# Two buffers each for q and for its pairs, swapped by batch with the scaled nodes and with the raw and turned tiles

## The chip, the cores and the metric

One core of one Trainium2 chip runs the whole program. The metric is the device time of one execution in microseconds. Three executions of the kernel before took 14094.63, 14094.72 and 14200.6 us; their median is 14094.72 us.

## The reference, cut to what matters

```python
# x: (8, 2048, 128), adj: (8, 2048, 2048), all float32
def gnn(x, adj, W, b):                       # layers 0, 2 and 3, up to details of the degree
    d = degree(adj) ** -0.5
    return (d[:, :, None] * adj * d[:, None, :]) @ x @ W + b

def attention(x, adj, WQ, WK, p):            # layer 1
    q, k = x @ WQ, x @ WK
    h = relu(q[:, None, :, :] + k[:, :, None, :])
    score = einsum('bijd,d->bij', h, p)      # 8 x 2048 x 2048 scores, 128 features each
    return softmax(score + where(adj > 0, 0, -1e22)) @ x

x = layernorm(x + layer(x))                  # four times: layer 0, 1, 2, 3
```

The cost is in `h`: for each of the 8 x 2048 x 2048 pairs of nodes, 128 features are added, clipped at zero and summed with the weights p.

## The kernel before, in words

**Layout of the attention.** q of a batch lies in SBUF with the features on the 128 partitions and the 2048 nodes in the row. A "row" of work is one instruction over 128x2048: for one node i, max(q, -k_i) or relu(q + k_i). One block is 128 nodes i (t = 0 to 15 within a batch), cut into 32 groups g of four rows (u = 0 to 3). A place is one group of one block, so a batch has 512 places.

**Two kinds of row.** In 20 of the 32 groups (kind D), VectorE (DVE) takes the max from `q_pair`, in which each 32-bit word holds q as a high and a low float16. In the other 12 (kind A: g = 2, 5, 7, 10, 13, 15, 18, 21, 23, 26, 29, 31), ScalarE (ACT) takes the relu from `q_f32`. Both write to a ring of two groups in `big`. TensorE (PE) multiplies each finished group with a window of weights into the four PSUM banks of `score` (`score_rows`): 32 matmuls of float16 for a D group, 16 of float32 for an A group. DVE and ACT can be at most two groups of their kind ahead of PE. One row of the block, group 1 with u = 3 (`POOL_ROW`), is computed by GpSimd (POOL) in place of DVE, wherever `has_pool_row` says so.

**The end of a block.** After group 31, DVE adds the mask to the four banks and takes the maximum of each (`masked_scores`, L968 and L972). It frees the banks for group 0 of the next block. `masked_at` says where in the next block this stands in DVE's order. ACT takes the exponentials at place 5 (L760); their transposes and the product with x follow at later places.

**Side work.** Into the same order of places the kernel puts, for other batches: the transposition of adj (`raw` is loaded by half rows, PE turns it, ACT copies it to `turned`, SyncE stores it; 32 units, 7 half units each block, from t = 0 on), two sums per half row on ACT (`sum_unit`), the three layers with products of `gs` (the scaled nodes) and pieces of the turned adj (`layer2` from block 2, `layer3` from 6, `layer0` from 10), and q, k and their pairs for the next batch at the end of `layer0` (blocks 11 to 15; stored to DRAM).

**Batches.** A round c runs the attention of batch c + 1, layers 2 and 3 of batch c, and layer 0 and the transposition of batch c + 2. `OPENING` (-2) and `CLOSING` (8 - 1) have side work only, `FIRST` is -1. There are eight rounds with attention, hence seven changes of batch. There `load_q` loads `q_f32` and `q_pair` (1 MB each). All transfers of the program are issued in order by SyncE (SP), which waits on semaphores before each.

**What the change touches.** `load_q` (L530), its call at the end of the round, `load_raw` (L396), `masked_at` and `has_pool_row` with `pool_rows`, `scale_nodes` (L870), and every use of `q_f32`, `q_pair`, `gs`, `raw` and `turned` (those become functions of the round). The functions:

Of the kernel before, what the change touches and what calls it, by code (L numbers as in the profile page):

```python
# [24 lines left out]
def halves(words):  # L25

    return words[:, :].bitcast(F16).rearrange("p (n e) -> p n e", e=2)
# [3 lines left out]
def build(nc, x, adj, w0, b0, wq, wk, p, w2, b2, w3, b3, out):  # L31
# [50 lines left out]
    with ExitStack() as ctx:  # L82
# [8 lines left out]
        q_f32 = sb("q_f32", [P, N])  # L91
        q_pair = sb("q_pair", [P, N])
# [9 lines left out]
        x1_turned, q_new = raw[:, 0:BANK], raw[:, BANK:2 * BANK]  # L102
        k_new = x1_turned
        stage = turned[:].rearrange("p m n -> p (m n)")
        high, pair_new = stage[:, 0:BANK], stage[:, BANK:2 * BANK]
# [6 lines left out]
        w_raw, squares = gs[:, 0, :], gs[:, 2:4, :]  # L112
# [122 lines left out]
        def masked_at(t):  # L235
            return (0, 0) if t == 0 else (1, 1)
# [134 lines left out]
        def _(sp):  # L371
# [23 lines left out]
            def load_raw(c, u):  # L395
                b = c + 2  # L396
                if u == 0:
                    sp.wait_ge(q_stored, qk_step(c + 1, STEPS) * 16)
                    sp.wait_ge(k_stored, qk_step(c + 1, STEPS) * 16)
                    sp.wait_ge(pair_stored, split_of(c + 1, STEPS, 0) * 16)  # L400
                else:
# [3 lines left out]
                sp.dma_start(raw[:], half_rows(b, u)).then_inc(raw_loaded, 16)  # L405
# [52 lines left out]
            def store_qk(c, place):  # L458
                b = c + 2
                for s in qk_at(c, place, "q_store"):  # L460
                    sp.wait_ge(turn_free[1], turn_use(c, ("q", s)) + 1 + AHEAD)
                    sp.dma_start(q_kept[b, :, s * BANK:(s + 1) * BANK], q_new).then_inc(q_stored, 16)
                for s in qk_at(c, place, "k_store"):
                    sp.wait_ge(turn_free[1], turn_use(c, ("k", s)) + 1 + AHEAD)
                    sp.dma_start(k_blocks[:, bass.ds(b * T + s * PER, PER), :],
                                 k_new.rearrange("p (t n) -> p t n", n=P)).then_inc(k_stored, 16)
                for i, what in enumerate(("q_pair_store", "k_pair_store")):
                    for s in qk_at(c, place, what):
                        sp.wait_ge(low_written, split_of(b, s, i) + 1)
                        sp.wait_ge(high_written, split_of(b, s, i) + 1)  # L470
                        if i == 0:
                            dst, src = q_pair_kept[b, :, s * BANK:(s + 1) * BANK], pair_new
                        else:
                            dst = k_pair_blocks[:, bass.ds(b * T + s * PER, PER), :]
                            src = pair_new.rearrange("p (t n) -> p t n", n=P)
                        sp.dma_start(dst, src).then_inc(pair_stored, 16)

            def side(c, place):
                for u in units_where(c, lambda u: evict_place(2 * u + 1) + 1 == place):
                    sp.wait_ge(turn_free[1], turn_use(c, ("unit", u, 1)) + 1 + AHEAD)  # L480
                    store_turned(c + 2, u, turned[:]).then_inc(turned_stored, 16)
# [60 lines left out]
            def attention(c):  # L542
# [15 lines left out]
                if not one_of(c, LAST):  # L558
                    load_q(c + 1)
# [673 lines left out]
```

## Time and profile before

| what | us |
|---|---|
| median of three executions | 14094.72 |
| the profiled execution | 14105.47 |
| its span, first to last instruction | 14103.7 |
| DVE busy | 13362.3 (95%) |
| ACT busy | 13096.3 (93%) |
| PE busy | 13010.3 (92%) |
| POOL busy | 902.7 (6%) |

Three engines are busy for over 90% of the span, so none of them can be read alone: what bounds a stretch has to be found by the stretch. A profile line gives the busy time of a group of instructions and the idle time of its engine before them, with what ended that idle time. A timeline row gives start, length, engine, line and the number of equal instructions merged; the number in square brackets is the idle time before it.

### The profile page before, as it was taken

How to read it: one execution, taken by the hardware profiler on the slowest of the kernel's cores; microseconds unless marked ns; L12 is line 12 of the kernel's file. 1: busy time of each engine (PE TensorE's matmuls, PEld its weight loads, DVE VectorE, ACT ScalarE, POOL GpSimd, SP SyncE). 2: the span in 40 equal slices, each digit the busy share in tenths (PEclk: the TensorE clock that was granted, in tenths of full speed). 3: DMA queues.
4: the chain of work that ended last, by engine and by line, in shares of the span. 5: the costliest groups of instructions: out<-in, count | busy, mean ns of one | idle time of the engine just before them, and what ended most of it. 6: DMA issues, size and time to landing. Idle time of an engine off the chain costs nothing.

```text
span 14103.7 us, 317692 instructions
## 1 busy us (share of the span) xinstructions
PE 13010.3 (92%) x143877; PEld 5491.8 (39%) x143877; DVE 13362.3 (95%) x14048; ACT 13096.3 (93%) x8612; POOL 902.7 (6%) x615
## 2 busy tenths in 40 slices
PE   6889989999899998999989999899989999899988
PEld 3333334443344433443334443344433444333333
DVE  6999999999999999999999999999999999999995
ACT  5999999999999999999999999999999999999994
POOL 0000000000000000001000000000000010000000
PEclk8999999999999999999999999999999999999999
DMA  5111112221122112221122211222112221011103
GB/s 186 45 51 47 49 53 85 86 62 51 55 86 88 61 41 64 88 86 58 40 71 85 86 57 39 73 82 85 60 36 75 89 79 57 30 49 51 43 12 109
DMA packets 714329, 935.45 MB, mean 66 GB/s; under 512 B 61712, under 2 KB 455952, under 8 KB 693520
## 3 DMA queue, kind: packets, MB, share of 16 engines
q1 hardware_dynamic: 712976, 915.13, 20.8%
q8 instruction: 1128, 18.48, 0.5%
q14 instruction: 225, 1.84, 0.0%
HBM read 722.01 MB, written 184.55 MB: 64 GB/s over the span
## 4 chain that ended last, share of the span: by engine, by line
DVE 45%; PE 38%; ACT 13%; issue 2%; DMA 1%; SPq 0%; POOL 0%; DVEq 0%; POOLq 0%; ACTq 0%
DVE big L1019 40%; PE score L1165 28%; ACT big L783 11%; PE acc L1086 5%; PE acc L1145 2%; PE turn L1063 2%; DVE att L968 2%; DVE gx L898 1%; DMA piece<-adj_turned 1%; ACT y_turned L706 0%; ACT turned L696 0%; DMA big<-in_adj_dram 0%; DVE stats L904 0%; PE acc L1092 0%; PE turn L1116 0%
## 5 line engine op out<-in xcount | busy, mean ns | idle before, releaser
L1019 DVE TENSOR_SCALAR big<-q_pair,k_pair_cols 128x2048 f32<-128x2048 f32 x10120 | 12213.0, 1279 | 407.3 <-PE score L1165 391.3
L783 ACT ACTIVATE big<-q_f,k_cols 128x2048 f32<-128x2048 f32 x6144 | 11790.3, 1998 | 297.7 <-PE score L1165 253.1
L1165 PE MATMUL score<-big,unit_window 128*32 128x512 f16 x81920 | 5192.0, 397 | 772.7 <-DVE big L1019 735.8
L1165 PE MATMUL score<-big,sign_window 128*32 128x512 f32 x49152 | 5624.8, 598 | 187.6 <-ACT big L783 185.1
L1165 PEld LDWEIGHTS score<-big,unit_window 128*32 128x32 bf16 x81920 | 2301.1, 96 | 3914.0 <-issue 1204.7
L1165 PEld LDWEIGHTS score<-big,sign_window 128*32 128x32 f32 x49152 | 1570.0, 111 | 3515.7 <-issue 3016.3
L1086 PE MATMUL acc<-piece,gs 128*128 128x512 f32 x3072 | 1444.8, 598 | 36.8 <-DVE gs L881 22.1
L1086 PEld LDWEIGHTS acc<-piece,gs 128*128 128x128 f32 x3072 | 532.5, 191 | 546.9 <-issue 456.3
L607 POOL TENSOR_SCALAR att_var<-att_mom 128x1 f32<-128x1 f32 x128 | 66.9, 523 | 10020.2 <-DVE att_mom L986 10020.2
L1145 PE MATMUL acc<-x,att_turned 128*128 128x128 f32 x4096 | 555.4, 279 | 0.0
L1145 PEld LDWEIGHTS acc<-x,att_turned 128*128 128x128 f32 x4096 | 498.9, 192 | 56.6 <-issue 56.6
L764 ACT ACTIVATE att_turned<-turn 128x512 f32<-128x512 f32 x512 | 299.1, 584 | 126.0 <-PE turn L1063 125.9
L618 POOL TENSOR_SCALAR big<-q_pair,k_pair_cols 128x2048 f32<-128x2048 f32 x120 | 236.7, 1972 | 2708.9 <-DVE bank_max L968 2708.9
L968 DVE CUSTOM_DVE_ANT_0 att<-score,att 128x512 f32<-128x512 f32 x512 | 325.9, 684 | 42.3 <-PE score L1165 41.2
L696 ACT ACTIVATE turned<-turn 128x512 f32<-128x512 f32 x448 | 260.2, 581 | 109.4 <-PE turn L1063 109.4
L760 ACT ACTIVATE att<-att,neg_max 128x2048 f32<-128x2048 f32 x128 | 255.8, 1998 | 104.4 <-DVE neg_max L972 104.4
L1063 PEld LDWEIGHTS turn<-ident,att 128*128 128x128 f32 x2048 | 216.0, 141 | 332.6 <-issue 327.5
L1063 PE MATMUL turn<-ident,att 128*128 128x128 f32 x2048 | 337.6, 288 | 3.8 <-ACT att L760 3.1
L1063 PE MATMUL turn<-ident,raw 128*128 128x128 f32 x1792 | 277.7, 278 | 29.9 <-DMA raw<-in_adj_dram 29.8
L1063 PEld LDWEIGHTS turn<-ident,raw 128*128 128x128 f32 x1792 | 204.4, 141 | 120.8 <-issue 83.9
L709 ACT ACTIVATE y_turned<-raw 128x1024 bf16<-128x1024 f32 x224 | 237.0, 1058 | 7.1
L720 ACT ACTIVATE y_turned<-acc 128x512 f32<-128x512 f32 x96 | 55.9, 583 | 196.0 <-PE acc L1086 196.0
(89 smaller groups left out, 2697.5 us busy)
## 6 DMA issues: line engine op xcount, KB each, us to landing
piece<-adj_turned SPq DMA_DIRECT2D x1536, 256.0 KB, 2.8
att<-in_adj_dram SPq DMA_DIRECT2D x128, 1024.0 KB, 5.2
raw<-in_adj_dram SPq DMA_DIRECT2D x224, 512.0 KB, 4.8
adj_turned<-turned SPq DMA_DIRECT2D x224, 512.0 KB, 4.7
big<-in_adj_dram SPq DMA_DIRECT2D x32, 512.0 KB, 7.4
adj_turned<-big SPq DMA_DIRECT2D x32, 512.0 KB, 6.9
gx<-in_x_dram SPq DMA_DIRECT2D x32, 256.0 KB, 4.3
q_kept<-raw SPq DMA_DIRECT2D x32, 256.0 KB, 3.7
```

What stands on the lines that cost most here:

```text
L618: pool.tensor_scalar(ring["D"][:, RANK[g] % RING * 4 + u, :], q_pair[:], 3.0e38, k_pair_cols[:, t % 2, QUAD * u + g:QUAD * u + g + 1], ALU ...
L696: nc.scalar.activation(stage[:, k * BANK:(k + 1) * BANK], turn[1][:], ACT.Copy).then_inc(turn_free[1], 1)
L709: nc.scalar.activation(unread, raw[:], ACT.Abs, accum_out=abs_part[:, u % 2, u // 2:u // 2 + 1]).then_inc(raw_abs_summed, 1)
L760: nc.scalar.activation(att[:], att[:], ACT.Exp, bias=neg_max[:], accum_out=row_sum[:]).then_inc(exp_ready, 1)
L764: nc.scalar.activation(att_turned[:, cc % 2, :], turn[0][:], ACT.Copy).then_inc(turn_free[0], 1)
L783: ins = nc.scalar.activation(ring["A"][:, RANK[g] % RING * 4 + u, :], q_f32[:], ACT.Relu, bias=k_cols[:, t % 2, QUAD * u + g:QUAD * u + g ...
L968: nc.vector.tensor_tensor_reduce(out=part, in0=score[:, cc, :], in1=part, scale=1.0, scalar=-3.0e38, op0=ALU.add, op1=ALU.max, accum_out=b ...
L1019: ins = nc.vector.tensor_scalar(ring["D"][:, RANK[g] % RING * 4 + u, :], q_pair[:], k_pair_cols[:, t % 2, QUAD * u + g:QUAD * u + g + 1], ...
L1063: ins = nc.tensor.transpose(turn[k][:, j * P:(j + 1) * P], src(j), ident[:])
L1086: nc.tensor.matmul(acc[1][:], gs[:, i, :], piece[:, i % PIECES, :], start=(i == 0), stop=(i == T - 1)) \
L1145: ins = nc.tensor.matmul(acc[0][:, 0:D], att_turned[:, cc % 2, j * P:(j + 1) * P], x1[:, cc * PER + j, :], start=(cc == 0 and j == 0), sto ...
L1165: ins = nc.tensor.matmul(score[QUAD * u:QUAD * (u + 1), cc, :], window[:, QUAD - 1 - g:2 * QUAD - 1 - g], row, start=(g == 0 and part == 0 ...
```

## The change

The buffers `gs`, `raw` and `turned` are gone. There are two of q (`q_bufs`) and two of its pairs (`pair_bufs`), with the same total size. In round c the attention reads number (c + 1) mod 2 of each. The other q buffer holds the scaled nodes, the other pair buffer holds `raw` in its first half and the turned tiles in its second. `load_q` for the next round is issued at place 21 of block 15, and no longer after the end of the round. `load_raw` of unit 0 waits for the last DVE and POOL rows of the round before. The masked scores of the last block of a batch stand where those of all blocks stand, after the first row of group 1, and POOL has its row in block 0 too, except in the first batch.

```diff
-        q_f32 = sb("q_f32", [P, N])
-        q_pair = sb("q_pair", [P, N])
+        q_bufs = [sb(f"q_f32_{i}", [P, N]) for i in range(2)]
+        pair_bufs = [sb(f"q_pair_{i}", [P, N]) for i in range(2)]
...
-        gs = sb("gs", [P, T, D])
-        raw = sb("raw", [P, HALF])
-        turned = sb("turned", [P, HALF_TILES, P])
...
+        def q_of(b):
+            return q_bufs[b % 2][:]
+        def pairs_of(b):
+            return pair_bufs[b % 2][:]
+        def scaled(c):
+            return q_bufs[c % 2][:].rearrange("p (t f) -> p t f", f=D)
+        def raw(c):
+            return pair_bufs[c % 2][:, 0:HALF]
+        def stage(c):
+            return pair_bufs[c % 2][:, HALF:N]
...
         def masked_at(t):
-            return (0, 0) if t == 0 else (1, 1)
+            return (1, 1)
...
         def has_pool_row(c, t):
-            return t > 0
+            return t > 0 or not one_of(c, FIRST)
         def pool_rows(c, t):
-            return (c + 1) * (T - 1) + max(t - 1, 0)
+            return max(c * T + (T + t - 1), 0)
...
             def load_raw(c, u):
                 if u == 0:
                     ...
+                    if not one_of(c, FIRST):
+                        sp.wait_ge(rows_ready["D"], (c + 1) * (T * N_OF["D"]))
+                        sp.wait_ge(pool_row_ready, pool_rows(c, 0))
...
             def load_q(c):
                 sp.wait_ge(q_stored, qk_step(c + 1, STEPS) * 16)
+                sp.wait_ge(piece_used, piece_of(c - 1, "layer0", STEPS - 1, T, AHEAD))
+                sp.dma_start(q_of(c + 1), q_kept[c + 1]).then_inc(q_loaded, 16)
+                sp.wait_ge(k_stored, qk_step(c + 1, STEPS) * 16)
                 sp.wait_ge(pair_stored, split_of(c + 1, STEPS, 0) * 16)
-                if not one_of(c, FIRST):
-                    sp.wait_ge(rows_ready["A"], (c + 1) * (T * N_OF["A"]))
-                sp.dma_start(q_f32[:], q_kept[c + 1]).then_inc(q_loaded, 16)
-                if not one_of(c, FIRST):
-                    sp.wait_ge(rows_ready["D"], (c + 1) * (T * N_OF["D"]))
-                    sp.wait_ge(pool_row_ready, pool_rows(c, 0))
-                sp.dma_start(q_pair[:], q_pair_kept[c + 1]).then_inc(q_pair_loaded, 16)
+                sp.dma_start(pairs_of(c + 1), q_pair_kept[c + 1]).then_inc(q_pair_loaded, 16)
...
                         elif not one_of(c, LAST):
                             load_k(c + 1, 0)
+                            load_q(c + 1)
...
-                if not one_of(c, LAST):
-                    load_q(c + 1)
...
             def scale_nodes(c, name, s):
+                if name == "layer2":
+                    dve.wait_ge(rows_ready["A"], (c + 1) * (T * N_OF["A"]))
```

**SP's order at a change of batch.** The transfers of the kernel before, from the mask of block 15 to the first half rows of the new round:

```order
L550 DMA att<-in_adj_dram 128x2048
L425 DMA k_cols<-k_kept 128x128
L426 DMA k_pair_cols<-k_pair_kept 128x128
L456 DMA x_kept<-att_pre 128x128
L536 DMA q_f<-q_kept 128x2048
L540 DMA q_pair<-q_pair_kept 128x2048
L405 DMA raw<-in_adj_dram 128x1024 x2
```

The same stretch of the changed kernel, in which the name `q_pair` also stands for the raw half rows:

```order
L576 DMA att<-in_adj_dram 128x2048
L454 DMA k_cols<-k_kept 128x128
L455 DMA k_pair_cols<-k_pair_kept 128x128
L563 DMA q_f_1<-q_kept 128x2048
L566 DMA q_pair<-q_pair_kept 128x2048
L485 DMA x_kept<-att_pre 128x128
L434 DMA q_pair<-in_adj_dram 128x1024 x2
```

The two loads of q now stand behind those of k, ahead of the store of the block before (`x_kept`), and no transfer but that store is left between them and the raw half rows.

**DVE's order at a change of batch.** The last rows of block 15, the masked scores and the rows of the new batch, before:

```order
L1019 TENSOR_SCALAR big<-q_pair,k_pair_cols 128x2048 x4
L968 ISA att,bank_max<-score,att 128x512
L968 ISA bank_max 128x1
...
L972 TENSOR_REDUCE neg_max<-bank_max 128x1
L1019 TENSOR_SCALAR big<-q_pair,k_pair_cols 128x2048 x60
L957 TENSOR_SCALAR att<-att 128x2048
```

And in the changed kernel:

```order
L1046 TENSOR_SCALAR big<-q_pair,k_pair_cols 128x2048 x9
L995 ISA att,bank_max<-score,att 128x512
L995 ISA bank_max 128x1
...
L999 TENSOR_REDUCE neg_max<-bank_max 128x1
L1046 TENSOR_SCALAR big<-q_pair,k_pair_cols 128x2048 x54
L984 TENSOR_SCALAR att<-att 128x2048
```

Five rows of the new batch moved ahead of the masked scores (4 became 9), and one of the 60 behind them is no longer DVE's (54 are left): it is POOL's.

## Rows read from the trace of the kernel before

**Rows 1.** The page's busy time by engine: us, share of the span, instructions.
```profile
PE 13010.3 (92%) x143877; PEld 5491.8 (39%) x143877; DVE 13362.3 (95%) x14048; ACT 13096.3 (93%) x8612; POOL 902.7 (6%) x615
```

**Rows 2.** Waits of the whole span: us in total, times, longest.
```profile
ACT big L783 <- DMA q_f<-q_kept: 43.7, 8, 9.3
...
DVE big L1019 <- DMA q_pair<-q_pair_kept: 12.5, 2, 11.8
```

**Rows 3.** Timeline of SP, third change of batch: start, length, line, transfer.
```profile
5323.94 0.33 SPq L550 DMA_DIRECT2D att<-in_adj_dram  x1
...
5324.81 0.43 SPq L426 DMA_DIRECT2D k_pair_cols<-k_pair_kept  x1
...
5359.92 0.32 SPq L536 DMA_DIRECT2D q_f<-q_kept  x1
5361.94 0.32 SPq L540 DMA_DIRECT2D q_pair<-q_pair_kept  x1
5362.37 0.37 SPq L405 DMA_DIRECT2D raw<-in_adj_dram  x1
```

**Rows 4.** Timeline of DVE, third change of batch.
```profile
5335.55 1.22 DVE L957 TENSOR_SCALAR att<-att 128x2048 f32<-128x2048 f32 x1
...
5347.25 9.63 DVE L1019 TENSOR_SCALAR big<-q_pair,k_pair_cols 128x2048 f32<-128x2048 f32 x8
...
5357.05 4.87 DVE L1019 TENSOR_SCALAR big<-q_pair,k_pair_cols 128x2048 f32<-128x2048 f32 x4
5365.24 0.69 DVE L968 CUSTOM_DVE_ANT_0 att<-score,att 128x512 f32<-128x512 f32 x1 [3.32 <-PE score L1165]
...
5368.55 44.35 DVE L1019 TENSOR_SCALAR big<-q_pair,k_pair_cols 128x2048 f32<-128x2048 f32 x37
```

**Rows 5.** Timeline of DVE, an ordinary block boundary (blocks 0 and 1).
```profile
5475.45 0.69 DVE L968 CUSTOM_DVE_ANT_0 att<-score,att 128x512 f32<-128x512 f32 x1
...
5478.09 16.82 DVE L1019 TENSOR_SCALAR big<-q_pair,k_pair_cols 128x2048 f32<-128x2048 f32 x14
```

**Rows 6.** Timeline of PE, third change of batch.
```profile
5358.76 3.62 PE L1165 MATMUL score<-big,sign_window 128*32 128x512 f32 x32
...
5364.01 3.61 PE L1165 MATMUL score<-big,sign_window 128*32 128x512 f32 x32
5369.76 1.12 PE L1063 MATMUL turn<-ident,raw 128*128 128x128 f32 x4 [2.14 <-DMA raw<-in_adj_dram]
...
5378.26 2.04 PE L1165 MATMUL score<-big,unit_window 128*32 128x512 f16 x32 [1.37 <-DVE big L1019]
...
5393.68 0.60 PE L1063 MATMUL turn<-ident,raw 128*128 128x128 f32 x4
```

**Rows 7.** Timeline of ACT, third change of batch.
```profile
5364.77 7.68 ACT L783 ACTIVATE big<-q_f,k_cols 128x2048 f32<-128x2048 f32 x4 [4.94 <-DMA q_f<-q_kept]
...
5377.05 15.27 ACT L783 ACTIVATE big<-q_f,k_cols 128x2048 f32<-128x2048 f32 x8
5394.32 0.60 ACT L696 ACTIVATE turned<-turn 128x512 f32<-128x512 f32 x1 [2.00 <-PE turn L1063]
...
5406.20 0.60 ACT L696 ACTIVATE turned<-turn 128x512 f32<-128x512 f32 x1 [1.01 <-PE turn L1063]
```

**Rows 8.** Blocks 0 and 1, third change: PE, PEld, DVE, ACT, POOL busy.
```profile
5368.00:5478.00 110.00, 93.39 (x1120) 39.15 (x1124) 107.28 (x102) 106.87 (x78) 3.61 (x3) 0.97 0.16 51
5478.00:5588.00 110.00, 96.09 (x1104) 39.57 (x1096) 104.85 (x101) 109.90 (x77) 5.63 (x4) 0.98 0.26 78
```

**Rows 9.** Timeline of DVE at the second and at the last change of batch.
```profile
3642.55 0.69 DVE L968 CUSTOM_DVE_ANT_0 att<-score,att 128x512 f32<-128x512 f32 x1 [4.54 <-PE score L1165]
...
12261.18 0.69 DVE L968 CUSTOM_DVE_ANT_0 att<-score,att 128x512 f32<-128x512 f32 x1 [4.63 <-PE score L1165]
```

**Rows 10.** POOL's row at the boundary of rows 5, and transfers: KB, us to landing.
```profile
5476.26 1.97 POOL L618 TENSOR_SCALAR big<-q_pair,k_pair_cols 128x2048 f32<-128x2048 f32 x1 [20.07 <-DVE bank_max L968]
...
raw<-in_adj_dram SPq DMA_DIRECT2D x224, 512.0 KB, 4.8
```

**Rows 11.** All DVE rows: ns min/median/max.
```profile
L1019 DVE TENSOR_SCALAR big<-q_pair,k_pair_cols x10120: 1251/1279/1302, 227.3 to 13912.8; 128x2048 f32<-128x2048 f32 x199
```

More of the change, by code:

```diff
@@ L111, in build, with x1_turned, q_new, high @@
         bias = {n: sb("bias_" + n, [P, P]) for n in ("layer0", "layer2", "layer3")}
-        w_raw, squares = gs[:, 0, :], gs[:, 2:4, :]
+        def q_of(b):
[8 more added lines that the diff above has]
+            return pair_bufs[c % 2][:, HALF:N]
+        def x1_turned(c):
+            return raw(c)[:, 0:BANK]
+        def q_new(c):
+            return raw(c)[:, BANK:2 * BANK]
+        k_new = x1_turned
+        def high(c):
+            return stage(c)[:, 0:BANK]
+        def pair_new(c):
+            return stage(c)[:, BANK:2 * BANK]
+        w_raw, squares = scaled(0)[:, 0, :], scaled(0)[:, 2:4, :]
         p_col = sb("p_col", [P, 1])
@@ L404, in load_raw @@
                     sp.wait_ge(raw_abs_summed, unit_of(b, u))
-                sp.dma_start(raw[:], half_rows(b, u)).then_inc(raw_loaded, 16)
+                sp.dma_start(raw(c), half_rows(b, u)).then_inc(raw_loaded, 16)
             def load_piece(c, name, s, i):
@@ L695, in copy_unit @@
                 act.wait_ge(turn_full[1], turn_use(c, ("unit", u, k)) + 1)
[L696 removed]
+                nc.scalar.activation(stage(c)[:, k * BANK:(k + 1) * BANK], turn[1][:], ACT.Copy).then_inc(turn_free[1], 1)
             def sum_unit(c, u):
@@ L705, in sum_unit @@
                 act.wait_ge(raw_abs_summed, unit_of(c + 2, u))
-                nc.scalar.activation(unread, raw[:], ACT.Copy,
+                nc.scalar.activation(unread, raw(c), ACT.Copy,
                                      accum_out=deg_part[:, u % 2, u // 2:u // 2 + 1]).then_inc(raw_summed, 1)
                 act.wait_ge(raw_summed, unit_of(c + 2, u) + 1)
-                nc.scalar.activation(unread, raw[:], ACT.Abs,
+                nc.scalar.activation(unread, raw(c), ACT.Abs,
                                      accum_out=abs_part[:, u % 2, u // 2:u // 2 + 1]).then_inc(raw_abs_summed, 1)
@@ L782, in attention @@
                                 copy_weights(c * T + (T + t - 1), COPY_IN[g])
-                            ins = nc.scalar.activation(ring["A"][:, RANK[g] % RING * 4 + u, :], q_f32[:], ACT.Relu,
+                            ins = nc.scalar.activation(ring["A"][:, RANK[g] % RING * 4 + u, :], q_of(c + 1), ACT.Relu,
                                                        bias=k_cols[:, t % 2, QUAD * u + g:QUAD * u + g + 1])
@@ L1075, in turn_unit @@
                 pe.wait_ge(turn_free[1], turn_use(c, ("unit", u, k)) + AHEAD)
-                turn_four(1, lambda j: raw[:, (k * PER + j) * P:(k * PER + j + 1) * P])
+                turn_four(1, lambda j: raw(c)[:, (k * PER + j) * P:(k * PER + j + 1) * P])
             def add_piece(c, name, s, i):
@@ L1085, in add_piece @@
                            (s * (T // PIECES) + i // PIECES + 1) * 16)
-                nc.tensor.matmul(acc[1][:], gs[:, i, :], piece[:, i % PIECES, :], start=(i == 0), stop=(i == T - 1)) \
+                nc.tensor.matmul(acc[1][:], scaled(c)[:, i, :], piece[:, i % PIECES, :], start=(i == 0), stop=(i == T - 1)) \
                     .then_inc(piece_used, 1)
@@ L1091, in add_self @@
                 for j in range(PER):
-                    nc.tensor.matmul(acc[1][:, j * P:(j + 1) * P], gs[:, s * PER + j, :], ident[:], start=False, stop=False)
+                    nc.tensor.matmul(acc[1][:, j * P:(j + 1) * P], scaled(c)[:, s * PER + j, :], ident[:], start=False, stop=False)
             def project(c, name, s):
```

41 lines of the change are left out of this document (18 added, 23 removed).

## The prediction

> **What bounds the kernel now.** I began with the busy time by engine: DVE, ACT and PE are all busy for 92 to 95% of the span [rows 1], so no engine is the bound everywhere, and a gain on one of them counts only where the other two can follow. The list of waits comes next, since the change is about two loads. ACT waits for the load of q eight times, 43.7 us in all, and one of these is the 9.3 us at the very start; seven are left, of some 4.9 us. DVE waits for the pairs only twice [rows 2]. So the load costs DVE nothing directly at the seven changes of batch. What it costs DVE is seen in the third view, the timelines around one change of batch. I took the third; five of the seven look like it, the second and the last have a longer wait of DVE.
>
> DVE ends its last row of block 15 at 5357.05 + 4.87 = 5361.92 us. It can't take a row of the next batch, since the masked scores stand first in its order, and it idles 3.32 us until PE has multiplied the last groups [rows 4]. PE's last group, g = 31, ends at 5364.01 + 3.61 = 5367.62. The masked scores then run behind PE bank by bank and the first row of the new batch starts at 5368.55. At an ordinary boundary the same scores stand behind the first row of group 1, DVE does not wait at all, and they take 5478.09 - 5475.45 = 2.64 us [rows 5] against 5368.55 - 5365.24 = 3.31 here [rows 4]. ACT waits 4.94 us for q [rows 7]. PE waits for the raw half rows, which are queued behind both loads [rows 3, 6].
>
> Which engine carries the time on from there: in block 0 DVE is busy for 107.28 of 110 us, in block 1 ACT for 109.90 of 110 [rows 8]. So a gain at a change of batch is kept only if DVE has it in block 0 and ACT in block 1.
>
> **The change, part by part**, at the third change of batch.
>
> *Masked scores behind five rows.* A row costs 9.63 / 8 = 1.20 us in a run of rows [rows 4], five of them 6.0. They now start at 5361.9 and end at 5367.9, after PE's last group, so the scores start at once, take 2.64 us and end at 5370.6. Before, DVE had done scores and five rows at 5368.55 + 6.0 = 5374.6. DVE is 4.0 us earlier. This is the idle time of 3.32 and the 0.67 by which the scores ran slower.
>
> *POOL's row in block 0.* It takes one row of 1.20 us from DVE. POOL starts it when the first bank has been read and needs 1.97 us, within DVE's 2.64 us of scores [rows 5, 10]; it is done when DVE has finished them, and the group also needs two more rows of DVE. So it delays nobody, and if that cover were gone it would cost at most its 1.97 us a change. DVE's gain is 4.0 + 1.2 = 5.2 us, and PE's group 1 starts at 5378.26 - 5.2 = 5373.1 [rows 6].
>
> The 1.97 us need a weighing. The row shows POOL starting while DVE does scores, and DVE's next row begins at 5478.09, 0.14 us before POOL ends at 5478.23 [rows 5, 10]. The Trainium skill (SBUF — State Buffer, section "SBUF: two separate sides") says that DVE, in some of its fast modes, and GpSimd share a pair of ports as an exclusive lock: who comes second waits for the whole instruction of the first. By that rule the row in block 0 would be free as long as it starts beside the scores and could cost up to a whole row if it slipped out of them; the measured boundary shows no such loss.
>
> *The load of q.* ACT can start its group 2 once PE has used group 29, at 5358.76 + 3.62 = 5362.4 [rows 6], in place of 5364.8: 2.4 us earlier. Later in block 0 ACT waits for PE's transposes, 2.00 and 1.01 us [rows 7]; PE comes to them 5.2 us earlier, so ACT can use up these waits: 2.4 + 3.0 = 5.4 us. That is just over the 5.2 of DVE and PE. The smaller of the two holds: **5.2 us** at ACT as well when block 1, ACT's, begins.
>
> *The raw half rows.* They are issued when DVE and POOL have done the last rows, at about 5362, as before, but with no megabytes ahead of them. At the median of 4.8 us to landing [rows 10] they are there at 5367.2, and PE ends group 31 at 5367.6. PE's wait of 2.14 us goes [rows 6]. It was beside DVE's path, so I book nothing for it, but without it DVE's gain would have met this wait next.
>
> *The two loads at place 21 of block 15.* SP comes there at 5325.2 and has nothing more to issue until the store of the block before, over 30 us later [rows 3]. The new waits in front of the loads are for things stored and used at earlier places. The loads may slow the mask of block 15, issued 1.3 us earlier and needed by DVE at 5335.55, 11.6 us after its issue [rows 3, 4]. At the change before, q, pairs and the first raw half rows, 2.5 MB, came between 5359.92 and 5369.76 [rows 3, 6]. At this rate all 3 MB take 11.8 us. So even a mask that came last of all would cost 0.2 us, and one that comes first nothing. I take nothing. By the Trainium skill (DMA: Bandwidth & Descriptors, section "Queues, rings and completion order") each engine takes the descriptors of a ring in order, so that the mask would come first; the sum would be the same or 1.4 us better than the bound.
>
> *The new wait of the scaled nodes of layer 2* is for ACT's rows of the batch before. It stands in block 1, over a block later: nothing. Semaphores and address changes elsewhere: nothing, the instructions are the same.
>
> *The other changes.* At the second one DVE idles 4.54 us [rows 9], but the round that follows is no longer than the others, so I take 5.2 there too. At the last one it idles 4.63 [rows 9] and there is no transposition in the round that follows, hence less for ACT and PE: 4.63 + 0.67 + 1.20 = 6.5 us. The first round has no change. **Sum: 6 x 5.2 + 6.5 = 37.7 us.** The profiled execution takes 14105.47 us, so it would be 14067.8. The median of the runs is 10.8 us below it; I expect a median of 14094.7 - 37.7 = **14057 us**, 0.27% less. A change under 1% can hardly be told from none in a measurement of this kernel, whose three runs lie 106 us apart.
>
> **The rivals.**
>
> *ACT's own gain is all that lasts* (0.16). If the waits of 2.00 and 1.01 us are caused by something else than DVE's lateness, ACT keeps 2.4 us. For it: block 1 is ACT's alone. Against it: PE itself waits for DVE between the change and these transposes, 1.37 us ahead of group 1 [rows 6]. 7 x 2.4 = 17 us: 14078.
>
> *More than forecast* (0.08). If DVE's whole gain lasts at each change, as 6.5 at the last, 7 x 6.5 = 45.5 us: 14049. For it: the second change has a wait as long as the last's. Against: ACT has only 5.4 to give.
>
> *The mask or the k columns come late* (0.06). A wait for the mask in place of the one for q. At most 0.2 us by the rate above, 2 us if the loads ran at half of it and only part of the delay fell on the mask: 14 us back, 14071.
>
> *The change does not do what it says* (0.05). SP could be held at the new place, by a wait for the last stored pairs, and issue the loads late. The gap of 30 us on SP speaks against it. It would leave things near 14090.
>
> *Rows become slower* (0.04), the case on the other side. All rows now read buffers whose neighbours in the same allocation are written by DMA and ACT and read by PE. If that cost anything it would fall on every DVE row. It decides from 37.7 us / 10120 rows = 3.7 ns a row on. All rows lie between 1251 and 1302 ns, the median is 1279 [rows 11]; at the slowest value, 23 ns more, it is 233 us, and the time would be 14290. Against it: the narrow band of 51 ns holds while transfers of all kinds go on.
>
> *The forecast*, 33 to 42 us gained: 0.61.
>
> **How the numbers follow.** The likeliest case gives 14057. The range takes in the forecast, ACT's gain alone (14078), the larger gain (14049) and the late mask, with some 5 us for the offset between a profiled run and a median, which is known from one profile only: 14042 to 14083. It leaves out the two last rivals and part of the rest. Only the slower rows reach 1%: faster by over 1% 0.01, within 1% 0.96, slower by over 1% 0.03.
>
> **What would show it.** In the changed profile: no wait of ACT for q but the first, of 9 us; no wait of DVE for PE ahead of the masked scores at the seven changes; POOL with 127 rows for 120 and DVE with 10113 for 10120; group 1 of the new batch some 5 us earlier after DVE's last row; no wait of PE for raw half rows there; the waits of ACT for the first transposes gone or below 1 us. The prediction is wrong if DVE's wait turns up again within block 0 or 1 in another place, if the mask of block 15 becomes a wait, or if the mean row differs from 1279 ns by more than 3 ns.

## The result, and the profile after

| | median, us | runs |
|---|---|---|
| before | 14100.33 | 20, 14094.52 to 14200.6 |
| changed | 14062.95 | 20, 14053.85 to 14070.68 |

The ratio is 0.9973, with a 95% interval from 0.9967 to 0.9978: 31 to 47 us faster. By the medians it is 37.4 us, where the sum said 37.7. The time itself was forecast at 14057 and came out 6 us higher, which is nearly the 5.6 us by which three runs had put the median of before too low. One of the twenty executions of before took 14200.6 us, the other nineteen at most 14104.92.

The page's busy times of the changed kernel, which answer to [rows 1] (us, share of the span, instructions):

```profile
PE 13018.0 (93%) x143877; PEld 5506.2 (39%) x143877; DVE 13353.0 (95%) x14041; ACT 13099.3 (93%) x8612; POOL 912.9 (6%) x622
```

The profiled spans are 14103.7 us before and 14063.9 after, 39.8 less. DVE has 7 rows fewer and is busy for 13362.3 - 13353.0 = 9.3 us less. The remaining 30.5 us must be idle time of DVE. Here is its wait ahead of the masked scores, from the list of waits of the kernel before (engine, line, what it waited for: us in total, times, longest):

```profile
DVE att L968 <- PE score L1165: 41.2, 45, 4.9
```

And from the list of the changed kernel, with the two waits for q that answer to [rows 2]:

```profile
DVE att L995 <- PE score L1192: 11.5, 26, 5.0
...
DVE big L1046 <- DMA q_pair<-q_pair_kept: 12.2, 1, 12.2
...
ACT big L808 <- DMA q_f<-q_kept: 9.7, 1, 9.7
```

That is 41.2 - 11.5 = 29.7 us less, 28.0 of them at the seven changes of batch, where no wait ahead of the scores is left. So 39.0 of the 39.8 us are found on DVE: fewer rows, and no wait for the scores there. ACT's seven waits for q are gone; the one at the start is left.

The third change of batch in the changed kernel. SP's timeline (start, length, line, transfer) answers to [rows 3]:

```profile
5307.34 0.33 SPq L576 DMA_DIRECT2D att<-in_adj_dram  x1
...
5308.74 0.38 SPq L563 DMA_DIRECT2D q_f<-q_kept  x1
5309.22 0.38 SPq L566 DMA_DIRECT2D q_pair<-q_pair_kept  x1
5340.58 0.32 SPq L485 DMA_DIRECT2D x_kept<-att_pre  x1
5345.49 0.33 SPq L434 DMA_DIRECT2D q_pair<-in_adj_dram  x1
```

DVE's timeline answers to [rows 4]:

```profile
5340.46 10.86 DVE L1046 TENSOR_SCALAR big<-q_pair,k_pair_cols 128x2048 f32<-128x2048 f32 x9
5351.22 0.69 DVE L995 CUSTOM_DVE_ANT_0 att<-score,att 128x512 f32<-128x512 f32 x1
...
5353.79 0.16 DVE L999 TENSOR_REDUCE neg_max<-bank_max 128x1 f32<-128x4 f32 x1
5353.87 21.61 DVE L1046 TENSOR_SCALAR big<-q_pair,k_pair_cols 128x2048 f32<-128x2048 f32 x18
```

PE's and ACT's timelines answer to [rows 6, 7]:

```profile
5340.35 3.27 PE L1192 MATMUL score<-big,unit_window 128*32 128x512 f16 x32 [2.75 <-DVE big L1046]
5343.45 3.60 PE L1192 MATMUL score<-big,sign_window 128*32 128x512 f32 x32
...
5348.70 3.63 PE L1192 MATMUL score<-big,sign_window 128*32 128x512 f32 x32
5352.26 0.66 PE L1090 MATMUL turn<-ident,q_pair 128*128 128x128 f32 x4
5352.84 2.02 PE L1192 MATMUL score<-big,unit_window 128*32 128x512 f16 x32
5356.49 2.00 PE L1192 MATMUL score<-big,unit_window 128*32 128x512 f16 x32 [1.63 <-DVE big L1046]
```

```profile
5347.21 7.70 ACT L808 ACTIVATE big<-q_f,k_cols 128x2048 f32<-128x2048 f32 x4 [4.23 <-PE score L1192]
...
5359.51 15.27 ACT L808 ACTIVATE big<-q_f,k_cols 128x2048 f32<-128x2048 f32 x8
5374.67 0.59 ACT L721 ACTIVATE q_pair<-turn 128x512 f32<-128x512 f32 x1
```

The reader is to see four things. The nine rows run without a break and the scores follow at once: the wait of 3.32 us is gone. PE turns the raw half rows right after its last group, without a wait. ACT now waits for PE, not for q, and the wait is 4.23 us, not the 4.94 - 2.4 = 2.5 that the sum implied. The copy of the turned tile for which ACT had waited 2.00 us [rows 7] comes at 5374.67 without a wait, and so does the next.

**A yardstick for one change of batch.** The intervals of the ratios below reach some 11 to 20 us either way, which is too coarse for single terms. Within a trace there is a finer measure: the time from the end of the masked scores of block 14 (in block 15) to the end of those of block 0 (in block 1). It spans the change, both ends stand at the same place of the order in all kernels, and there are seven of them. It covers blocks 15 and 0, and not block 1. I read it from the timeline rows of the reduction to `neg_max` (L972, and its line in each kernel). For the third change it is 5478.02 - 5269.77 = 208.25 us before and 5457.27 - 5252.60 = 204.67 after.

| kernel | seven changes, us | sum | against before |
|---|---|---|---|
| before | 208.3 209.5 208.2 208.3 209.0 208.4 206.7 | 1458.4 | |
| changed | 204.4 203.0 204.7 204.9 205.0 203.0 200.1 | 1425.1 | -33.3 |

The other 6.5 us of the 39.8 lie between the changes, 4.6 of them in the first batch, whose order of instructions the change leaves alone: 1822.3 us before, 1817.8 after. In the trace of the kernel before with POOL's row alone, whose first batch is that of before, the same stretch takes 1819.3, and in that of the changed kernel with the scores first 1823.3. So these 4.6 us are chance of the two profiles, and so probably is the rest. A gain of 37.4 by the medians and of 33.3 in the stretches are then two measures that agree only to some 4 us.

### The profile page after: what moved, and what is told of

It is laid out like the page before. It is cut to its first block, busy times and chain, and to the rows that moved or that the text cites. A ratio compares the mean times of both kernels' runs of the same rounds, so it can differ in the third digit from the quotient of the medians.

```text
span 14063.9 us, 317752 instructions
## 1 busy us (share of the span) xinstructions
PE 13018.0 (93%) x143877; PEld 5506.2 (39%) x143877; DVE 13353.0 (95%) x14041; ACT 13099.3 (93%) x8612; POOL 912.9 (6%) x622
## 4 chain that ended last, share of the span: by engine, by line
DVE 43%; PE 37%; ACT 16%; issue 3%; DMA 1%; SPq 0%; POOL 0%; DVEq 0%; POOLq 0%; ACTq 0%
DVE big L1046 39%; PE score L1192 27%; ACT big L808 14%; PE acc L1113 5%; PE acc L1172 2%; PE turn L1090 2%; DVE att L995 2%; DMA piece<-adj_turned 1%; DVE gx L925 1%; ACT y_turned L731 1%; ACT q_pair L721 1%; DMA big<-in_adj_dram 0%; DVE stats L931 0%; PE acc L1119 0%; ACT att L785 0%
## 5 line engine op out<-in xcount | busy, mean ns | idle before, releaser
L1046 DVE TENSOR_SCALAR big<-q_pair,k_pair_cols 128x2048 f32<-128x2048 f32 x10113 | 12208.6, 1283 | 408.3 <-PE score L1192 392.0
L1113 PE MATMUL acc<-piece,q_f 128*128 128x512 f32 x3072 | 1444.1, 598 | 37.7 <-DVE q_f L908 22.0
L1113 PEld LDWEIGHTS acc<-piece,q_f 128*128 128x128 f32 x3072 | 534.0, 191 | 545.7 <-issue 459.8
L785 ACT ACTIVATE att<-att,neg_max 128x2048 f32<-128x2048 f32 x128 | 255.9, 1999 | 106.0 <-DVE neg_max L999 106.0
L721 ACT ACTIVATE q_pair<-turn 128x512 f32<-128x512 f32 x448 | 260.8, 582 | 94.9 <-PE turn L1090 94.6
L995 DVE CUSTOM_DVE_ANT_0 att<-score,att 128x512 f32<-128x512 f32 x512 | 324.8, 688 | 11.9 <-PE score L1192 11.5
L1090 PE MATMUL turn<-ident,q_pair 128*128 128x128 f32 x1792 | 277.0, 277 | 18.5 <-DMA q_pair<-in_adj_dram 18.5
L1090 PEld LDWEIGHTS turn<-ident,q_pair 128*128 128x128 f32 x1792 | 204.0, 141 | 109.0 <-issue 89.0
L734 ACT ACTIVATE y_turned<-q_pair 128x1024 bf16<-128x1024 f32 x224 | 237.0, 1058 | 7.1
```

The lines of the kernel that those rows point to most:

```text
L721: nc.scalar.activation(stage(c)[:, k * BANK:(k + 1) * BANK], turn[1][:], ACT.Copy).then_inc(turn_free[1], 1)
L734: nc.scalar.activation(unread, raw(c), ACT.Abs, accum_out=abs_part[:, u % 2, u // 2:u // 2 + 1]).then_inc(raw_abs_summed, 1)
L785: nc.scalar.activation(att[:], att[:], ACT.Exp, bias=neg_max[:], accum_out=row_sum[:]).then_inc(exp_ready, 1)
L995: nc.vector.tensor_tensor_reduce(out=part, in0=score[:, cc, :], in1=part, scale=1.0, scalar=-3.0e38, op0=ALU.add, op1=ALU.max, accum_out=b ...
L1046: ins = nc.vector.tensor_scalar(ring["D"][:, RANK[g] % RING * 4 + u, :], pairs_of(c + 1), k_pair_cols[:, t % 2, QUAD * u + g:QUAD * u + g ...
L1090: ins = nc.tensor.transpose(turn[k][:, j * P:(j + 1) * P], src(j), ident[:])
```

## The experiments

All were timed beside the kernel before, and profiled. "Stretch" is the sum of the yardstick, 1458.4 us before and 1425.1 in the changed kernel.

**Without POOL's row in block 0.**

```diff
         def has_pool_row(c, t):
-            return t > 0 or not one_of(c, FIRST)
+            return t > 0
...
```

`pool_rows`, which counts these rows for the semaphores, goes back with it.

> The changed kernel without POOL's row in block 0: DVE has all 80 rows there again. Theory A (the sum as predicted: DVE's gain counts in full, because ACT can follow): 7 rows of 1.20 us are lost, so 8.4 us of the 37.4 us gain go, and the time is about 29 us under the kernel before. Rival B (at most changes ACT is what limits the gain after the change: DVE is idle 4 us in block 0 of the changed kernel at changes 1, 3, 4 and 5, against 2.7 us before): the row is worth 1.2 us only at changes 2, 6 and 7, and the time is 2 to 4 us over the changed kernel, some 34 us under the kernel before.

14074.16 us, ratio 0.9981 (0.9973 to 0.9990): 27.2 us under before. Stretch 1430.1, so the row is worth 5.0 us there and 11 us by the medians, whose intervals do not tell these two from A's 8.4 or B's 2 to 4. The single changes say more. Without the row the seven take 204.8, 204.3, 204.7, 204.9, 204.6, 204.7 and 202.1 us; the changed kernel gained on this 1.3, 1.7 and 2.0 us at changes 2, 6 and 7 and -0.4 to 0.4 at 1, 3, 4 and 5. That is B's pattern. Why these changes differ is found under "ACT's 2.4 us" below.

**Early loads alone:** as above, and the scores first again.

```diff
         def masked_at(t):
-            return (1, 1)
+            return (0, 0) if t == 0 else (1, 1)
```

> The changed kernel with the masked scores of a batch's last block ahead of the new batch's rows, as in the kernel before, and no POOL row in block 0: only the early loads are left. Theory A (DVE carries the time into the new batch): DVE still idles 3.3 us or more ahead of the scores, PE gets group 0 as late as before, and the gain is 0 to 7 us. Rival B (the load of q is what costs): ACT starts 2.4 us earlier at each change and this lasts, 17 us gained. Rival C: the earlier raw half rows and ACT's start together give more, up to 25 us.

14103.05 us against 14101.39, ratio 1.0001 (0.9991 to 1.0010). Stretch 1457.6. A holds, B and C fall. The timelines at the third change, DVE and then ACT:

```profile
5352.26 4.87 DVE L1046 TENSOR_SCALAR big<-q_pair,k_pair_cols 128x2048 f32<-128x2048 f32 x4
5360.46 0.69 DVE L995 CUSTOM_DVE_ANT_0 att<-score,att 128x512 f32<-128x512 f32 x1 [3.33 <-PE score L1192]
```

```profile
5357.76 7.69 ACT L808 ACTIVATE big<-q_f,k_cols 128x2048 f32<-128x2048 f32 x4 [2.69 <-PE score L1192]
```

Both q's are in SBUF, ACT starts 2.2 us earlier than before, counted from DVE's last row, where 2.4 were reckoned, and nothing comes of it: DVE idles as long as before. The step from this kernel to the one without POOL's row is one line, the place of the scores. It moves the median by 28.9 us and the stretch by 27.5: **seven times 3.9 us**.

**q late for ACT, pairs early for DVE.**

```diff
+            def load_q_late(c):
                 sp.wait_ge(q_stored, qk_step(c + 1, STEPS) * 16)
                 sp.wait_ge(piece_used, piece_of(c - 1, "layer0", STEPS - 1, T, AHEAD))
+                if not one_of(c, FIRST):
+                    sp.wait_ge(rows_ready["A"], (c + 1) * (T * N_OF["A"]))
                 sp.dma_start(q_of(c + 1), q_kept[c + 1]).then_inc(q_loaded, 16)
...
+                if not one_of(c, LAST):
+                    load_q_late(c + 1)
...
```

The call stands behind the last place of the round. `load_q` keeps the load of the pairs and its place.

> The changed kernel with only the load of q for ACT put back to the end of the round, behind ACT's last row; the pairs for DVE stay early, the scores stay behind five rows, POOL has its row. ACT should wait about 4.9 us for q at each change, 0.7 to 2.4 us more than for PE's ring slot in the changed kernel. Theory A: ACT has 3.0 us of later waits in block 0, which cover most of it; the loss against the changed kernel is the amount by which ACT's gain falls under DVE's 5.2 us, about 2 us a change at six changes and nothing at the last, 13 us in all, so some 25 us under the kernel before. Rival B (ACT does not limit): no loss, 37 us under the kernel before. Rival C (the load of q was the point of the change): nearly all is lost, within 5 us of the kernel before.

14071.74 us, ratio 0.9980 (0.9972 to 0.9989): 29.7 us under before, 8.8 over the changed kernel. Stretch 1430.1, 5.0 over it. ACT waits 4.8 to 5.0 us for q. The first six changes take 204.9 to 205.1 us. So A's 2 us are lost at changes 2 and 6, where the changed kernel takes 203.0, and 0 to 0.5 at the four where it takes 204.4 to 205.0. The last, where ACT does not limit, is 200.1 in both. A's mechanism holds in the traces, its 13 us were too much; the interval alone, 16 to 39 us under before, does not exclude B. The early load of q for ACT is a small part of the change.

**Pairs late for DVE, q early for ACT.** The same edit on the other load, whose wait is for the last rows of DVE and POOL.

> The changed kernel with only the load of the pairs for DVE put back behind DVE's last row of the round; q for ACT stays early, the masked scores stay behind five rows, POOL has its row. Theory A (the scores can be moved only because the pairs are there early): DVE waits for the pairs at each change, 5.4 to 6.2 us from its last row, then does five rows, then the scores, which end at about 6 + 6 + 2.6 = 14.8 us after the last row; in the kernel before scores and five rows took 6.6 + 6.0 = 12.6. So each change is 2 us later than before, and with POOL's row, beside DVE's first ones, 0 to 1.7 us worse: 14 to 26 us over the kernel before, 14116 to 14128. Rival B (DVE's order does not matter, the load of q is the gain): as the changed kernel, 14063.

14098.60 us against 14099.35, ratio 1.0000 (0.9991 to 1.0008). The whole gain is gone, so moving the scores gains only with the pairs at hand, and B falls. But the loss that A gave did not come. DVE's timeline at the third change shows why:

```profile
5354.10 4.87 DVE L1054 TENSOR_SCALAR big<-q_pair,k_pair_cols 128x2048 f32<-128x2048 f32 x4
5363.99 6.07 DVE L1054 TENSOR_SCALAR big<-q_pair,k_pair_cols 128x2048 f32<-128x2048 f32 x5 [5.01 <-DMA q_pair<-q_pair_kept]
5369.97 0.68 DVE L1003 CUSTOM_DVE_ANT_0 att<-score,att 128x512 f32<-128x512 f32 x1
...
5372.61 13.24 DVE L1054 TENSOR_SCALAR big<-q_pair,k_pair_cols 128x2048 f32<-128x2048 f32 x11
```

From the last row's end (5358.97) to the end of the scores it is 13.6 us, 1.0 more than the 12.65 before and not 2. The pairs, without q's megabyte ahead of them, landed 4.8 to 4.9 us after their issue at the seven changes, where the kernel before needed 5.4 to 7.3. POOL's row, here beside the scores, takes another row of 1.2 us from DVE; that would make up for the 1.0, and the stretch at this change is 208.1 for 208.2 before. No run took the row out of this kernel.

**POOL's row alone**, in the kernel before (`has_pool_row` and `pool_rows` of the change, nothing else).

> The kernel before with one part of the change alone: POOL takes its row in block 0 too (not in the first batch). Theory A (block 0 is DVE's): 7 x 1.20 = 8.4 us gained. Rival B: ACT limits, since it has waited 4.9 us for q and its later waits in block 0 are 3.0 us; these cover 1.2 us, so B gives the same here, and only if these waits are not DVE's doing is nothing gained. Rival C (the port that DVE and POOL share costs): the row is computed beside the scores, as in all blocks, so no loss.

14103.07 us against 14101.39, ratio 1.0002 (0.9993 to 1.0011): the expected 8.4 us do not show, though the interval does not exclude them, and the stretch is 1462.7, 4.3 longer. POOL's and then DVE's timeline at the second change:

```profile
3642.11 2.99 POOL L618 TENSOR_SCALAR big<-q_pair,k_pair_cols 128x2048 f32<-128x2048 f32 x1 [18.23 <-DMA q_pair<-q_pair_kept]
```

```profile
3641.35 0.16 DVE L972 TENSOR_REDUCE neg_max<-bank_max 128x1 f32<-128x4 f32 x1
3641.97 8.98 DVE L1019 TENSOR_SCALAR big<-q_pair,k_pair_cols 128x2048 f32<-128x2048 f32 x6 [0.47 <-DMA q_pair<-q_pair_kept]
```

POOL could start only when the pairs had landed, and by then DVE had started its own rows. POOL's row took 2.99 us for 1.97, and DVE's six rows 8.98 us where six take 7.3: one came 1.7 us late. At three more changes (1, 3 and 5) POOL started 0.4 to 0.5 us ahead of DVE's first row; it kept its length, and that row of DVE took 2.5 to 2.7 us for 1.27. The third, POOL and DVE:

```profile
5368.44 1.97 POOL L618 TENSOR_SCALAR big<-q_pair,k_pair_cols 128x2048 f32<-128x2048 f32 x1 [17.09 <-DMA q_pair<-q_pair_kept]
```

```profile
5368.98 6.09 DVE L1019 TENSOR_SCALAR big<-q_pair,k_pair_cols 128x2048 f32<-128x2048 f32 x4
```

Four rows take 6.09 us there for 4.87. At changes 4, 6 and 7 POOL's row was done before DVE's rows began. So Rival C's premise, the row beside the scores, failed at four changes.

**POOL's row beside the scores, but the scores first.** The changed kernel with `masked_at` alone put back.

> The changed kernel with only the masked scores of a batch's last block put back ahead of the new batch's rows: early loads and POOL's row in block 0 stay. In the kernel before with POOL's row alone, nothing was gained: the row started when the pairs had landed, beside DVE's first row, and DVE's next row came 2.4 us after it and not 1.2. Theory A (this lock ate the row's 1.2 us): here the pairs are there early, POOL computes its row beside the scores, and 7 x 1.2 = 8.4 us are gained, 14093. Rival B (the row's gain is lost at ACT or PE, not at the lock): no gain, 14101, like early loads alone. Rival C (all three parts need each other): between the two.

14100.52 us against 14102.24, ratio 0.9999 (0.9990 to 1.0008); stretch 1455.8, against 1457.6 without the row. POOL's row now takes 1.97 us at each change and DVE's next row is at most 0.2 us late, so the collision is gone, and still only 1.8 of the 8.4 us show in the stretch. The trace speaks against A: the collision ate part of the gain in the run before, but removing it does not bring the 8.4 us. The medians do not exclude A, whose 8.4 us lie within the interval. With the five rows in front, the row was worth 5.0 in the stretch. Part of this difference is TensorE's clock, as the table in the next section shows; the rest stays open.

**POOL's row apart from the scores.**

```diff
-        POOL_ROW = (1, 3)
+        POOL_ROW = (6, 3)
```

> The changed kernel with POOL's row moved from group 1, where it is computed beside the masked scores, to group 6, where DVE computes rows. The number of rows is the same. Theory A (DVE's rows and POOL's row lock each other out): in every block one DVE row comes 1.2 to 2 us late, 127 times; in the blocks that DVE bounds (14, 15 and 0 of each batch, all of the last, some 35) this lengthens the time, 40 to 80 us in all over the changed kernel; in the others DVE's idle time of 4 to 6 us covers it. Rival B (no lock; the gap in the run before came from something else): the same time as the changed kernel within 5 us, and all DVE rows 1.2 us apart.

14302.55 us, ratio 1.0142 (1.0128 to 1.0156): 240 us over the changed kernel, with the same work. The direction is A's, the size is three to six times its range. The line of POOL's rows in this kernel (ns min, median, max), and the line of DVE's rows:

```profile
L643 POOL TENSOR_SCALAR big<-q_pair,k_pair_cols x127: 2944/7452/12232, 347.2 to 14017.0; 128x2048 f32<-128x2048 f32 x127
```

```profile
L1046 DVE TENSOR_SCALAR big<-q_pair,k_pair_cols x10113: 1251/1280/3004, 227.9 to 14100.5; 128x2048 f32<-128x2048 f32 x199
```

In the changed kernel the same row of POOL takes 1.967 to 1.993 us. Beside DVE's rows it takes 2.9 to 12.2, and each time two to nine rows of DVE overlap it. It gets through only when a row of DVE has ended and no other is under way, and at 25 of the 127 it then holds up the next one, which takes up to 3.0 us instead of 1.28. What I had left out is that POOL is late by a median of 5.5 us and PE needs its row for the group: PE waits for it 29 times, 90.6 us in all. Where DVE carries the time, this comes back to DVE. In the last batch four blocks in a row, in which the changed kernel leaves DVE idle for 0.14 us, take 99.5 us each there and 105.6 to 106.2 here, with DVE idle for 6.1 to 6.6.

The Trainium skill (SBUF — State Buffer, "SBUF: two separate sides") describes an exclusive lock: who starts first, DVE in some of its fast modes or GpSimd, has the shared ports for the whole instruction, and the other is blocked. The four changes with POOL's row alone agree, with 2.5 to 3.0 us for the row that came second. In this run POOL's row waited over several instructions of DVE, which is longer than that rule says; here the measurement decides.

**Copies of turned tiles given from ACT to DVE**, to see what bounds blocks 0 to 2 of the changed kernel. The edit lets DVE do some of the copies out of PSUM, at the places that `DVE_COPIES` gives for each block. DVE's `copy_unit` waits for the same semaphores as ACT's:

```diff
+        DVE_COPIES = {0: (10,), 1: (10, 14, 18), 2: (14, 18)}
...
+            def copy_unit(c, u, k):
+                dve.wait_ge(turned_stored, unit_of(c + 1, u) * 16)
+                dve.wait_ge(turn_full[1], turn_use(c, ("unit", u, k)) + 1)
+                nc.vector.tensor_copy(stage(c)[:, k * BANK:(k + 1) * BANK], turn[1][:]).then_inc(turn_free[1], 1)
```

> The changed kernel with six of the turned tiles' copies out of PSUM in each round given from ACT to DVE: one in block 0, three in block 1, two in block 2. Theory A (after the change ACT bounds blocks 0 and 1, where it is idle for 0.1 us and DVE for 3 to 5): each copy takes 0.48 us from ACT, so a round is 1.4 to 2.4 us shorter, 10 to 17 us over seven rounds, and the time is about 14050. Rival B (DVE's idle time is spent in waits for PE that the copies do not fit into, so rows come later): no gain or 5 to 10 us lost.

14051.89 us, ratio 0.9965 (0.9952 to 0.9977): 11 us under the changed kernel by the medians, 50 under before. Stretch 1416.0, 9.1 shorter. A holds. The stretches of blocks 0 and 1 at the third change, first in the changed kernel, then in this one (PE, PEld, DVE, ACT, POOL busy; granted clock), answer to [rows 8]:

```profile
5354.00:5457.00 103.00, 90.83 (x1096) 37.40 (x1092) 99.39 (x92) 102.87 (x76) 2.29 (x4) 0.98 0.17 54
5457.00:5565.00 108.00, 93.97 (x1103) 39.14 (x1096) 102.85 (x100) 107.90 (x76) 5.90 (x4) 0.98 0.25 79
```

```profile
5348.00:5450.00 102.00, 91.35 (x1100) 37.53 (x1096) 100.46 (x99) 101.87 (x75) 3.03 (x4) 0.98 0.16 55
5450.00:5555.00 105.00, 92.41 (x1095) 38.25 (x1088) 103.81 (x101) 104.91 (x72) 5.56 (x4) 1.00 0.27 81
```

In the changed kernel ACT is busy to 0.1 us in both blocks: block 0, which was DVE's before, is ACT's after, at four of the six changes with side work. At changes 2 and 6 ACT is idle for 0.2 us and DVE for the 2.7 us that it had before, so there the two end together. With three copies fewer, block 1 takes 105.1 to 105.2 us at the six changes with side work, for 106.0 to 107.8.

The same with other sets, `{0: (10, 18), 1: (6, 10, 14, 18)}` and `{0: (10,), 1: (10, 14, 18)}`:

> The changed kernel with copies of turned tiles given to DVE in blocks 0 and 1 only, but more of them: two in block 0 and four in block 1. With one, three and two (block 2) the trace showed block 1 at 105.1 us for 107 and block 0 at 101.7 for 102.4 to 104.4, DVE still idle for 1.2 and 1.5 us there, block 2 not shorter. Theory A (ACT bounds the two blocks until DVE has no idle time left): another 1 us at most a round, so 5 us under the run with six copies, some 14047. Rival B (DVE is at its end with them): the same or up to 5 us longer, 14052 to 14057.

> The changed kernel with one copy in block 0 and three in block 1 given to DVE, none in block 2. Theory A (block 2 is PE's, which is idle for 2.7 us there, so its two copies were worth nothing): the same time as with them, 14052. Rival B (they were worth their 0.48 us each): 7 us longer, 14059.

The first took 14047.42 us, ratio 0.9965 (0.9952 to 0.9979), the second 14055.10, ratio 0.9970 (0.9958 to 0.9981). The differences among the three are 3 to 8 us and cannot be told from none by the medians. The traces say more. In that of the first, block 1 takes 104.4 to 104.5 us at the six changes with side work, for 105.1 to 105.2 with three copies, and DVE is idle for 0.2 us in it and ACT for 0.1: A's further gain of 0.7 us a round is there, and with it both engines are at their end. The yardstick, 1415.5 for 1416.0, does not cover block 1. In the trace of the second, block 2 takes 111.0 to 111.1 us at changes 3 to 6 as in the kernel with two more copies there, so these were worth nothing, as its A says; its median lies between A and B. By the medians the three are faster than the changed kernel by 8 to 16 us, with intervals that overlap its own, and faster than before by 44 to 52.

## Why the prediction was right, and where it was not

**The scores behind five rows: right, and most of it.** 4.0 us a change were forecast. At the third change DVE went from 5361.92 to 5374.6 before, 12.65 us for scores and five rows; now it takes from the end of the fourth row, 5340.46 + 10.86 - 6.02 = 5345.3, to 5353.87, 8.6 us. That is 4.1 less. The experiment that moves this line alone gives 3.9 a change on average, 27.5 us of the 33.3 in the stretches.

**The early loads: right in kind.** They earn nothing by themselves, and the moved scores earn nothing without the early pairs. The rival "ACT's own gain is all that lasts" falls: with the loads alone, ACT's gain does not last at all.

**ACT's 2.4 us: mis-sized at four changes.** The step took PE's group 28 at 2.01 us, as in the third change of before. In the changed kernel it ran at 3.27 us there. The granted clock of that stretch is the lower level, 1.2 GHz (the last but two number of the row):

```profile
5340.00:5343.00 3.00, 2.65 (x28) 1.03 (x32) 3.00 (x5) 2.98 (x2) 0.00 (x0) 0.50 0.08 22
```

I call this a dip. PE had been idle for 2.75 us just before, waiting for DVE. But it had been so ahead of the same group at every change, before and after, 2.75 to 2.79 us, and at some of them the clock stayed up, as at the sixth of the changed kernel (PE, then ACT):

```profile
10501.68 2.01 PE L1192 MATMUL score<-big,unit_window 128*32 128x512 f16 x32 [2.79 <-DVE big L1046]
```

```profile
10507.27 5.80 ACT L808 ACTIVATE big<-q_f,k_cols 128x2048 f32<-128x2048 f32 x3 [2.68 <-PE score L1192]
```

With the dip group 28 takes 2.8 to 3.5 us, and ACT's ring slot comes up to 1.5 us later. So ACT's wait is 4.2 to 4.3 us at five of the changes (1, 3, 4, 5 and 7) and 2.7 at the two others (2 and 6). Before, the dip lay on group 28 at changes 2 and 7, which is where the waits of 4.54 and 4.63 us came from [rows 9]; I had taken these as properties of the changes. At changes 1, 3, 4 and 5 ACT could then give 0.7 + 3.0 = 3.7 us and not 5.4, and the stretches there are shorter by 3.4 to 4.0, not by 5.2. At change 6, with no dip before or after, it is 5.4; at change 2, with a dip before, 6.5; at the last 6.6 (forecast 6.5), of which 1.3 are the dip of before. Four of the seven terms were too large in these two profiles, together by 6 us.

One profile of each kernel does not show where the dips fall in the other executions. That the sum of 37.7 meets the 37.4 of the medians within a microsecond, and not the 33.3 of the stretches, is therefore in part luck; it would follow if most executions had fewer dips at group 28 than the profiled one, which no run shows.

The dips also blur the experiments. Here are the stretches of a change (us), sorted by whether group 28 had a dip; the last change stands alone, since no transposition follows it.

| kernel | without dip | with dip | last change |
|---|---|---|---|
| before | 208.2 to 209.0 (1, 3 to 6) | 209.5 (2) | 206.7 |
| POOL's row alone | 208.5 to 210.3 (1 to 3) | 209.1 to 210.6 (4 to 6) | 206.3 |
| early loads alone | 208.2 to 208.3 (1 to 3, 5, 6) | 209.6 (4) | 206.7 |
| scores first, with the row | 207.7 to 208.0 (1, 2, 5) | 208.5 to 209.2 (3, 4, 6) | 205.7 |
| without POOL's row | 204.6 to 204.8 (1, 3, 5, 6) | 204.3, 204.9 (2, 4) | 202.1 |
| q late | 205.0 (3) | 204.9 to 205.1 (1, 2, 4 to 6) | 200.1 |
| changed | 203.0 (2, 6) | 204.4 to 205.0 (1, 3 to 5) | 200.1 |

Without a dip the change gains 5.2 to 5.4 us against the 208.2 to 208.4 of changes 1, 3, 4 and 6 of before, which is the forecast term.

**POOL's row: a cost of nothing was right, the gain mis-sized.** 8.4 us were forecast, 1.2 at each change; 5.0 came by the stretch, 11 by medians with wide intervals. By the table the row is worth 1.6 to 1.8 us without a dip and nothing that can be told from 0 with one, where ACT is what limits; at the last change it is worth 2.0. With the scores first it is worth 0.2 to 1.1, and this smaller value stays open. The row costs nothing only since the pairs are in SBUF before the scores begin. In the kernel before it met DVE's rows. The text had weighed this with an upper bound of one row of POOL, 1.97 us a change. The row apart from the scores shows this bound to be too low by far where DVE's rows follow without a break: 6 us a block in the four blocks named there, and 240 / 127 = 1.9 us on average over all blocks, also those in which DVE is not the bound.

**Raw half rows, mask, SP: right.** PE's wait is gone. The loads of q landed 8.2 and 10.0 us after their issue in the median, and DVE has no wait for the mask. SP issued them 1.4 us after the mask, as it had been free to. The mask of block 15 landed 4.8 to 5.3 us after its issue at the seven changes and q for ACT 8.8 to 10.0 us after that same moment: the mask came first, as the prediction took from the order of the ring.

**A sign of being wrong that did appear.** The prediction would be wrong if DVE's wait turned up again within block 0. In part it did: at changes 1, 3, 4 and 5 DVE idles for 3.6 to 4.8 us in block 0 of the changed kernel, waiting for PE, where it had idled for 2.7 to 3.3 before. These 1 to 2 us are of the size by which the stretches there are longer than at changes 2 and 6, where ACT could follow.

**The rows did not become slower,** but the sign that I named for it did appear: the mean row of DVE went from 1279 to 1283 ns.

```profile
L1046 DVE TENSOR_SCALAR big<-q_pair,k_pair_cols 128x2048 f32<-128x2048 f32 x10113 | 12208.6, 1283 | 408.3 <-PE score L1192 392.0 <-DMA q_pair<-q_pair_kept 12.2
```

12208.6 us for 10113 rows are 1.207 us each, and 12213.0 for 10120 were 1.207 too. Rows overlap, and the pitch, not the length, is what a run of them costs. My threshold of 3 ns was put on the wrong number.

**Still open:** why POOL's row is worth less with the scores first than with the scores behind at the same clock; where the dips fall in executions without a profile, and with that how much of the 37.4 us is the forecast sum; and what the 1.9 us outside the changes and outside the first batch are.

## What to carry to other kernels

A buffer loaded earlier is worth what the engine that carries the time can do with it: here the loads alone gave nothing, and one line of order, five independent rows in front of a step that waits for another engine, gave about three quarters of the gain, and none of it without the early pairs. When several engines are above 90% busy, read at the place of the change which engine has no idle time, before and again after, since the bound moved from DVE to ACT in the very block that gained. When a difference of single microseconds is read from two traces, compare places with the same granted clock. Work for GpSimd beside VectorE's fast rows belongs where VectorE does something else, and it has to be there when that moment comes.

## What the runs showed of the hardware

A GpSimd row over 128x2048 float32 took 1.97 us beside VectorE's reductions out of PSUM. Beside an unbroken run of VectorE's rows over 128x2048 it took 2.9 to 12.2 us, in the median 7.5. Where it started 0.4 to 0.5 us before VectorE's first row it kept its 1.97 us; a VectorE row that met it took 2.5 to 3.0 us for 1.28.

After the same 2.75 to 2.79 us of idle time at the same place of the program, TensorE's granted clock fell to 1.2 GHz at some changes of batch and stayed at 2.4 GHz at others. A group of 32 matmuls took 2.8 to 3.5 us with the fall and 2.0 without, and single changes of batch became up to 2.0 us longer by it. Where these dips fell differed between profiles of nearly the same order of work.
